# A state scan between two expert mixtures: exponent products over 120 rows, a rebuilt preparation, three state buffers

## The reference

```
xn = rmsnorm(x); delta_lo, Bs, Cs = split(xn @ x_proj_w.T, [8, 8+64])
delta = softplus(delta_lo @ dt_proj_w.T + dt_proj_b);  A = -exp(A_log)       # [128, 64]
# the 2 x 1024 rows are cut into M = 32 chunks of 64 rows, and all chunks step together:
def step(h, (dt, bt, ct, xt)):                         # h: [M, 128 d, 64 n], 64 steps
    h = exp(dt[..., None] * A) * h + dt[..., None] * bt[:, None, :] * xt[..., None]
    return h, einsum('mdn,mn->md', h, ct)
x = x + (y + xn * D) @ out_proj_w.T
```

## Time and profile before

| | us |
|---|---|
| median of 3 runs (1643.73 to 1649.44) | 1645.05 |
| profiled execution | 1653.65 |
| its span | 1651.6 |
| stage d, relu mixture (892.3 to 1022.1) | 129.8 |
| scan, preparation and first steps (1022.1 to 1157.4) | 135.3 |
| scan, the other steps (1157.4 to 1496.9) | 339.5 |
| mixture f (1496.9 to 1651.6) | 154.7 |

### The profile page before, as it was taken

One profiled execution on the slowest core, in us unless ns is written; L12 is line 12 of the kernel. 1 busy time (PEld: TensorE's weight loads), 2 busy tenths in 40 slices (PEclk: granted clock), 3 DMA queues, 4 the chain that ended last, 5 costly groups with the idle time before them and its releaser, 6 DMA issues.

```text
span 1651.6 us, 30294 instructions
## 1 busy us (share of the span) xinstructions
PE 1370.3 (83%) x11160; PEld 917.5 (56%) x11160; DVE 1037.8 (63%) x2050; ACT 958.5 (58%) x1507; POOL 649.1 (39%) x520
## 2 busy tenths in 40 slices
PE   4889996699999987889999996714888888877998
PEld 2667774344444434657666774413666666655676
DVE  5887766877777755786675445513666666665533
ACT  4667773166666676767675442534677677653433
POOL 2756656711222003756553002503566666661000
PEclk9999998699999997999999998755555555557999
DMA  4100000000000000010000000134111101110000
GB/s 139 53 25 1 0 1 1 1 1 2 2 0 1 1 1 26 26 53 1 0 1 1 1 0 0 21 69 73 46 26 25 25 22 25 31 53 1 1 0 25
DMA packets 34316, 32.20 MB, mean 19 GB/s; under 512 B 24200, under 2 KB 27672, under 8 KB 32536
## 3 DMA queue, kind: packets, MB, share of 16 engines
q1 hardware_dynamic: 34200, 30.64, 7.5%
HBM read 24.81 MB, written 5.82 MB: 19 GB/s over the span
## 4 chain that ended last, share of the span: by engine, by line
PE 56%; DVE 14%; ACT 13%; issue 8%; SPq 5%; POOL 2%; DMA 1%; DVEq 0%; POOLq 0%; ACTq 0%
PE ps L595 12%; PE ps L672 7%; PE ps L895 7%; PE ps L682 7%; ACT arena L1149 6%; PE ps L787 4%; PE ps L750 4%; PE ps L868 3%; PE ps L770 3%; DVE maxima L1667 3%; ACT hr L1038 2%; DVE xn L1468 2%; SPq L505 2%; PE ps L881 1%; SPq L499 1%
## 5 line engine op out<-in xcount | busy, mean ns | idle before, releaser
L1149 ACT ACTIVATE arena<-ps 128x512 f32<-128x512 f32 x256 | 244.5, 1080 | 116.4 <-PE ps L868 116.1
L1387 POOL TENSOR_TENSOR arena<-arena 128x512 f32<-128x512 f32 x126 | 223.4, 1793 | 194.9 <-PE ps L895 83.8
L1667 DVE TENSOR_REDUCE maxima<-ps 128x1 f32<-128x512 f32 (+3 forms) x320 | 190.3, 633 | 59.4 <-PE ps L753 39.9
L868 PE MATMUL ps<-arena 12*128 12x64 bf16 x2048 | 136.5, 236 | 101.0 <-DMA arena<-dt_parts 52.8
L595 PE MATMUL ps<-xp,wup 128*128 128x512 f32 (+1 forms) x768 | 207.8, 418 | 13.9 <-ACT hr L1038 10.0
L1411 POOL TENSOR_TENSOR hr<-arena,hr 128x512 fp32r<-128x512 f32 x128 | 173.7, 1363 | 93.8 <-ACT hr L1038 93.6
L595 PE MATMUL ps<-hr,wdn 128*128 128x512 f32 x768 | 201.3, 412 | 8.8 <-DVE hr L1570 7.3
L1104 ACT ACTIVATE arena<-ps 128x1024 f32<-128x1024 f32 (+1 forms) x192 | 150.5, 812 | 73.2 <-PE ps L770 37.0
L1038 ACT ACTIVATE arena<-ps 128x512 f32<-128x512 f32 x256 | 162.5, 635 | 51.0 <-PE ps L595 50.6
L868 PEld LDWEIGHTS ps<-arena 12*128 12x128 bf16 x2048 | 103.7, 121 | 157.1 <-ACT arena L1149 77.1
L595 PEld LDWEIGHTS ps<-xp,wup 128*128 128x128 f32 x768 | 148.3, 200 | 64.3 <-POOL wup L1398 16.4
(11 more groups left out here) (206 smaller groups left out, 2162.6 us busy)
## 6 DMA issues: line engine op xcount, KB each, us to landing
arena<-up_dram SPq DMA_DIRECT2D x16, 256.0 KB, 2.9
arena<-dn_dram SPq DMA_DIRECT2D x16, 256.0 KB, 3.2
arena<-up_dram SPq DMA_DIRECT2D x2, 1024.0 KB, 4.9
arena<-dn_dram SPq DMA_DIRECT2D x2, 1024.0 KB, 7.8
b_parts<-arena SPq DMA_DIRECT2D x16, 96.0 KB
dt_parts<-arena SPq DMA_DIRECT2D x8, 192.0 KB
u_parts<-arena SPq DMA_DIRECT2D x16, 96.0 KB
arena<-dt_parts SPq DMA_DIRECT2D x32, 48.0 KB
```

What stands on the lines that cost most here:

```text
L868: mm = e.matmul(ps[:, 4 + n % 2, j * 64:(j + 1) * 64], aw[32 * r:32 * r + KR, g0 + j, :], dts[k % 2][32 * r:32 * r + KR, g0 + j, :, th * T ...
L1149: e.activation(to.rearrange("p t m d -> p d m t"), ps[:, 4 + n % 2, :].rearrange("p (d m t) -> p d m t", d=DBK, t=TU), ACT.Exp, scale=-1.0 ...
L1387: e.tensor_tensor(hs[:, t % 2, cols], decay[:, u % 2, t4 * W + cols.start:t4 * W + cols.stop], hs[:, 1 - t % 2, cols], ALU.mult).then_inc( ...
L1667: e.tensor_reduce(maxf[:, at_max[0]:at_max[-1] + 1:max(1, at_max[-1] - at_max[0])], ps[:, n % 2, 0:ng * w].rearrange("p (g k) -> p g k", g ...
```

## The change

The diff touches only the scan, what GpSimd does in stage d, and what SP loads.

- The stationary tile of the exponent product has up to 120 rows (10 channels x 12 rows, zero outside the 12 rows of the channel) x 128, for each of the 128 channels; the moving tile holds the 10 channels' dt rows in one block of 120 rows. Products, columns and banks stay in number. `aw` grows from 4096 to 16384 bf16 a partition and is loaded by 60 DMAs in place of 24.
- The decay ACTIVATE reads the bank with a hop of 64 words from element to element and writes runs of 8 adjacent words.
- The input products of banks 2 and 3 are issued together, after the third addition of a step.
- The state has three buffers (t % 3); the multiply waits for the outputs of step t-3.
- POOL's memsets of `aw` and `czf` go to the head of stage d; that of bparts is gone.
- B is computed with padded weights `xpb`, so that its rows come out in the order of time; the splitting is shared out anew (POOL: B only; ACT: casts; DVE: subtractions), the skip product and the transposes of xn come later.
- The stores become few and large: one for b, one for dt, three small ones for the first dt chunk (dt0), two and two for u. The first dt chunk is fetched with two DMAs, further ones with 30 each; u and b are fetched in chunks of 4 steps with 24 DMAs.

The core of it:

```diff
         def spread_bank(e, n):
...
             for j in range(DBK):
-                mm = e.matmul(ps[:, 4 + n % 2, j * 64:(j + 1) * 64], aw[32 * r:32 * r + KR, g0 + j, :],
-                              dts[k % 2][32 * r:32 * r + KR, g0 + j, :, th * TU:(th + 1) * TU], start=True, stop=True)
+                d = q * DBK + j
+                nk = KR * min(DG, D - d // DG * DG)
+                of = dts[k % 2][0:nk, d // DG, :].rearrange("p (m t) -> p m t", t=TC)
+                mm = e.matmul(ps[:, 4 + n % 2, j * 64:(j + 1) * 64], aw[0:nk, d, :],
+                              of[:, :, th * TU:(th + 1) * TU], start=True, stop=True)
...
         def scan_tensor(e):
...
-                if t + 1 < NSTEP:
-                    e.wait_ge(SC["added"], 3 * t + 2)
-                    inputs(e, t + 1, (2,))
                 for n in todo[2:3]:
                     spread_bank(e, n)
                 e.wait_ge(SC["added"], 3 * t + 3)
                 if t + 1 < NSTEP:
-                    inputs(e, t + 1, (3,))
+                    inputs(e, t + 1, (2, 3))
                 state_out(e, t)
...
         def decay_bank(e, n):
...
-            to = decay[:, u % 2, :].rearrange("p (t m d) -> p t m d", t=TU, d=D)[:, :, :, d0:d0 + DBK]
-            e.activation(to.rearrange("p t m d -> p d m t"),
-                         ps[:, 4 + n % 2, :].rearrange("p (d m t) -> p d m t", d=DBK, t=TU), ACT.Exp,
+            to = decayf[u % 2].rearrange("p (t m d) -> p t m d", t=TU, d=D)[:, :, :, d0:d0 + DBK]
+            e.activation(to, ps[:, 4 + n % 2, :].rearrange("p (d m t) -> p t m d", d=DBK, t=TU), ACT.Exp,
                          scale=-1.0).then_inc(SC["decay_ready"], 1)
...
             def decay_state(t):
...
-                if t >= 2:
-                    e.wait_ge(SC["y_done"], t - 1)
+                if t >= 3:
+                    e.wait_ge(SC["y_done"], t - 2)
...
+            def relu_mixture_pool(e, st, nxt):
+                if nxt and nxt["kind"] == "scan":
+                    e.wait_ge(MX["y_read"], len(gelus) * NTB * E)
+                    e.memset(czf, 0.0).then_inc(SC["zeroed"], 1)
+                    e.memset(aw, 0.0).then_inc(SC["zeroed"], 1)
```

And SP's new fetches:

```diff
+                def fetch_dt(k):
+                    for dg in range(DG):
+                        ng = len(range(dg, D, DG))
+                        for c0, na in RUNS:
+                            r0 = KR * dg + 2 * c0
+                            sp.dma_start(dts[k % 2][r0:r0 + 2 * na, 0:ng, :],
+                                         scratch["dt"][dg::DG, k, 0:2 * na, :].rearrange("g r n -> r g n")
+                                         ).then_inc(dt_in[k % 2], 16)
...
+                fetch_inputs(0)
+                for m2 in range(2):
+                    sp.dma_start(scratch["u"][m2, TI:CHUNK].rearrange("t a b h n -> t a (b h n)"),
+                                 uparts[m2 * CHUNK + TI:(m2 + 1) * CHUNK]).then_inc(u_out, 16)
+                sp.wait_ge(u_out, 16 * 2)
+                fetch_inputs(1)
+                sp.wait_ge(dt_out, 16)
+                sp.wait_ge(SC["xn_turned"], NTB)
+                fetch_dt(1)
+                for k in range(2, NI):
+                    sp.wait_ge(SC["in_done"], 3 * TI * (k - 1))
+                    fetch_inputs(k)
+                    if k % 2 == 0 and k // 2 + 1 < NC:
+                        sp.wait_ge(SC["spread_done"], 2 * BKU * (k // 2))
+                        fetch_dt(k // 2 + 1)
```

More of the change, by code:

```diff
@@ new lines, in scan_tensor @@
+            turn_rows(0)
+            turn_rows(1)
+            low_rank(0)
+            turn_rows(2)
+            low_rank(1)
+            steps_of(0)
+            turn_rows(3)
+            low_rank(2)
+            steps_of(1)
+            low_rank(3)
+            steps_of(2)
+            rows_b(0)
+            rows_b(1)
+            steps_of(3)
+            rows_b(2)
+            rows_b(3)
+            for h in range(2):
+                e.wait_ge(SC["bf_ready"], h + 1)
+                for b in range(B):
+                    mm = e.matmul(ps[64 * b:64 * b + 64, 4 + h, :], xpw[:, RANK + STATE:RANK + 2 * STATE],
+                                  ut[:, b * S + h * 512:b * S + (h + 1) * 512], start=True, stop=True)
+                mm.then_inc(SC["bc_done"], 1)
@@ new lines, in scan_tensor @@
+            for g in range(NTB):
+                e.wait_ge(SC["z_added"], g + 1)
+                for j in range(TPB):
+                    mm = e.transpose(ps[:, g, j * P:(j + 1) * P], xn[:, TPB * g + j, :], ident[:])
+                mm.then_inc(SC["xn_turned"], 1)
+            for g in range(NTB):
+                e.wait_ge(SC["u_ready"], g + 1)
+                if g < 2:
+                    e.wait_ge(SC["cT_ready"], g + 1)
+                else:
+                    e.wait_ge(SC["bf_ready"], g + 1)
+                for j in range(TPB):
+                    mm = e.transpose(ps[:, 4 + g, j * P:(j + 1) * P], ut[:, (TPB * g + j) * P:(TPB * g + j + 1) * P], ident[:])
+                mm.then_inc(SC["u_turned"], 1)
@@ new lines, in dt_rest, with u_rest @@
+                def dt_rest(n, g):
+                    e.wait_ge(SC["dt_cast"], n * NTB + g + 1)
+                    for m2 in range(2):
+                        ins = e.tensor_tensor(dt_piece(1, g, m2), dt_piece(n, g, m2), dt_part(n, g, m2), ALU.subtract)
+                    ins.then_inc(SC["dt_rest"], 1)
+                def u_rest(n, g):
+                    e.wait_ge(SC["u_cast"], n * NTB + g + 1)
+                    of = ps[:, 4 + g, :] if n == 0 else urest[:, parts[g]]
+                    e.tensor_tensor(urest[:, parts[g]], of, uparts[:, n, parts[g]], ALU.subtract).then_inc(SC["u_rest"], 1)
@@ new lines, in scan_vector @@
+                z_add(0)
+                for g in range(1, NTB):
+                    z_add(g)
+                    z_size(g - 1)
+                z_size(NTB - 1)
+                for g in range(NTB):
+                    e.wait_ge(SC["ln_ready"], g + 1)
+                    e.scalar_tensor_tensor(out=zt[:, parts[g]], in0=zt[:, parts[g]], scalar=0.0, in1=soft[:, parts[g]],
+                                           op0=ALU.max, op1=ALU.add).then_inc(SC["dt_ready"], 1)
+                e.wait_ge(SC["bc_done"], NTB + 2)
@@ L1781, in scan_vector @@
+                for g in range(NTB):
+                    dt_rest(0, g)
+                    e.wait_ge(SC["dt_ready"], g + 1)
+                    e.tensor_tensor(ut[:, parts[g]], zt[:, parts[g]], ut[:, parts[g]], ALU.mult).then_inc(SC["u_ready"], 1)
+                for g in range(NTB):
+                    dt_rest(1, g)
+                for g in range(NTB):
+                    u_rest(0, g)
+                for g in range(NTB):
+                    u_rest(1, g)
                 e.wait_ge(SC["skip_done"], 1)
```

401 lines of the change are left out of this document (191 added, 210 removed).

## The result

The changed kernel takes 1535.03 us (median of 4 runs, 1533.68 to 1537.93) against 1647.24 of the kernel before on the same chip (4 runs, 1643.73 to 1653.22): ratio 0.9318, 95% interval 0.9285 to 0.9351, so 112 us or 6.8% less. Forecast were 1549 and 96. In the profiled executions the span fell from 1651.6 to 1532.9, by 118.7.

The account below looks back on a forecast made before the run. Scan steps of 5.59 us were taken as bound about equally by TensorE at half clock with its two-buffer wait and by ScalarE's banks. Gains 39 - 12 + 69 = 96 off 1645 gave 1549 us; 8-in-10 range 1520 to 1635.

Parts of the forecast that it names:

- Preparation and first stall: Scan's head until the second dt chunk lands: no memset holding VectorE, earlier casts, fewer SP transfers; gain 39 us.
- Memsets in the mixture: Stage before the scan: GpSimd's moved memsets hold a VectorE instruction and delay TensorE; loss 12 us, between 0 and 14.
- Exponent: Decay ACTIVATE on ScalarE: the new read and write pattern cuts a bank from 1083 ns to 0.64 to 0.70 us.
- slower rival: Decay ACTIVATE: hopping PSUM reads cost about 1.5 us a bank, 6.6 us a step, 1679 us in all; chance 0.07.
- second rival: Scan steps: exponent stays at 1.05 us, clock rises, ScalarE bounds at 4.75 us a step, 1567 us; chance 0.12.
- T: Time of one scan step, counted over 60.7 steps: from 5.59 to 4.45 us, a gain of 69 us.
- Clock: TensorE in the scan: 120-row exponent products lift the granted clock from 0.50 to near 1.00, at least mostly.
- sign in the kernel before: TensorE's clock fell to 0.50 during 8-row products and was back at 0.97 once 128-row products ran.
- first rival: Scan steps: clock stays at 0.50, exponent gets fast, TensorE bounds at 5.25 us a step, 1597 us; chance 0.22.
- Inputs together: Input products of banks 2 and 3 issued in one go on TensorE: zero gain, at worst 0.2 us a step lost.
- Gaps at changes of shape: TensorE switching between 120-row and 12-row products: up to 4 x 0.20 us more a step, less at high clock.
- end of a unit: Scan's multiply waiting for ScalarE's last bank of a unit: adds 0.3 to 0.5 us to a step.

Follow-up runs that it names:

- e5: Kernel before, with the decay ACTIVATE writing runs of 8 words and reading PSUM with a hop of 64 words: 1613.91 us, ratio 0.9798.
- e11: Kernel before, with the input products of banks 2 and 3 issued together after the third addition: 1655.70 us, ratio 1.0057.
- e9: Changed kernel, with the mixture's two memsets started later and the bf16 tile cleared through an fp32 view: 1518.82 us, ratio 0.9237.
- e1: Changed kernel, with the decay ACTIVATE back to reading PSUM in order and writing each word 8 KB apart: 1612.63 us, ratio 0.9778.
- e4: Changed kernel, with exponent products using only the first 12 rows, which computes something else: 1587.29 us, ratio 0.9636.
- e2: Changed kernel, with the input products of banks 2 and 3 issued apart again, as before the change: 1555.04 us, ratio 0.9432.
- e10: Changed kernel, with later memsets through an fp32 view, second dt chunk fetched first, five exponent banks in each of the first six steps: 1493.44 us, ratio 0.9068.
- e8: Changed kernel, with five exponent banks a step instead of four in the first six steps: 1511.18 us, ratio 0.9180.
- e6: Changed kernel, with the two memsets before the scan issued as 24 pieces of 512 fp32 words: 1531.67 us, ratio 0.9271.

## Why the prediction was right

The parts measured, 43.6 - 14.2 + 89.2, add up to 118.6 us between the two profiled executions; the medians differ by 112, and the forecast was 39 - 12 + 69 = 96.

*Preparation and first stall*, forecast 39, measured 43.6. Each link is there: the held tensor_scalar went (8.25 to 0.18 us), the parts of u were ready 10 us earlier from the head (59.5 to 49.6), the landing of u took 7.6 (taken as 8). Mis-sized was the fetch of dt: 30 at 0.34 and not 0.45, 3.3 us less, and its first chunk, 2.9 and not 4; the first 24 fetches of u and b took 9.9 and not 7.4, the last landing 1.6 and not 3. The first exponent product came at 1093.5 and not near 1080, behind the skip product's 32 matrix products (1088.2 to 1093.7); it cost nothing, since the steps wait for the second dt chunk. And the 8.25 us were those of one execution. In e5 and e11, which have the same preparation as the kernel before, the same instruction was let in between the first memset and the second:

```profile
1019.36 4.80 DVE L1759 TENSOR_SCALAR veps<-std 128x16 f32<-128x16 f32 x1
```

So 3.5 of the 43.6 us hang on the profiled execution, which is also one of the longer ones of its kernel (1653.65 us, median 1647.24).

*Memsets in the mixture*, forecast -12, measured -14.2. VectorE was held to the end of the second one; it was the tensor_scalar L1572 (at 894.2) and not the copy three instructions on, so that the loss came out a little over 12. In e9 the scan's head comes at 1019.9 for 1036.2: it was the whole loss.

*Exponent.* 0.64 to 0.70 forecast, 0.597 measured: the hop of 256 B in PSUM costs nothing that shows beside the plain pattern's 635 ns, and going from the old pattern to the new is worth 0.48 us an instruction. The slower rival did not come. But I mis-priced what hangs on it. I had put ScalarE at four times 1083 ns, 4.33 us a step; these instructions overlap at their ends, and 215.5 us for 56 steps are 3.85, so ScalarE's own sum was not what held the old step. And the second rival (long exponent, high clock) stood at T = 4.75 and 1567, where e1, the nearest to that case, is at 5.56 and 1613, at a clock of 0.66 and not a high one. I had taken the longest engine's sum for the step where two engines hand two banks to and fro, and had not seen that the clock would not rise far without the short exponent.

*Clock.* The direction was right, and e4 shows that the clock does not rise without the 120 rows; e1 shows that with them, but with the slow exponent, it gets to 0.66 only. The level (0.84, in alternation) was not near 1.00. The sign in the kernel before was weaker than I had read it: its products of 128 rows begin at 1044.9, and the clock stays at 0.50 until 1055. The first rival stood at T = 5.25 and 1597 (its terms, as written, add up to 5.19); e4, which is that case, has 4.97 and 1587.

*Inputs together*, forecast zero, is the term that failed: it is worth 20 us here (e2). I had judged it by order, not by which products can run side by side, nor by the two changes of kind that it saves.

*Gaps at changes of shape*, up to 4 x 0.20 us feared and less at the high clock: they came. In the starts of single products in the changed kernel's trace it is 0.13 us from the last 120-row product to the first of 12 rows and 0.15 back at the high clock (0.03 and 0.055 between two of a kind), 0.17 and 0.25 at the low one (0.05 and 0.11). That is some 0.1 us for each of the three such changes of a step, 0.3 a step. The timeline hides it, since the ends of products are modelled there: in e10 eight 12-row products start at 1203.96, 0.07 before the shown end of the 120-row ones begun at 1203.63. But sixteen 120-row products put off the next kind by 0.58 us (1205.30 to 1205.88) and eight by 0.33 (1203.63 to 1203.96): eight more cost 0.25, and the rest, 0.08, is the change. In e4, where exponents and inputs both have 12 rows, most changes show no such gap (0.01 to 0.05). The rule of the Trainium skill quoted above (TensorEngine Tiling (Array Packing), Key Properties) is borne out in kind by this; the 0.20 that I had set beside it stands in the trace at the weight load of L895, not at its products.

*T*, forecast 4.45, measured 4.12. The 89 us do not split into independent parts. The exponent's pattern alone gives 34 us (e5). Everything but that pattern gives nothing in the steps (e1, T = 5.56 for 5.59). Everything but the rows gives T = 4.97 (e4), 37 us. All together gives 89. Fast exponent and high clock each need the other: with 12 rows TensorE bounds at its low clock, and with the slow exponent the clock rises to 0.66 only and the hand-over takes the rest. What moved the sum from my 69 to 89 is the 20 of the inputs: without them (e2) T is 4.46, the 4.45 of the forecast. That this fits so well is in part luck. I had 0.3 to 0.5 for the end of a unit and a rest for additions and SP; in e2 the multiply waits 40.8 us for late banks, 0.68 a step, and the first addition 21.4 us for its inputs, 0.36. That SP would hold the steps did not happen: 48 fetches of u and b at 0.30 and 30 of dt at 0.33 make 3.1 us a step.

What would release the multiply was forecast wrongly: not the additions but the unit's last bank (20.5 us, 0.34 a step, which the sum had as the end of a unit). e8 removes it.

Open stays why the clock rises and falls just there in the steady part; the runs show the alternation and its dependence on the rows and on the exponent, no more. Open stays too why the runs of e6 lie so far apart (1517.9 to 1534.1). An execution in which VectorE is let in at an early seam of the memsets would be up to 9 us shorter, but the one of 1517.9 has no profile, so this is not shown.

## What to carry to other kernels

Where two engines pass a few buffers to and fro, price the hand-over and not the longer sum: e1 and the second rival differ by 46 us, for that and for the lower clock. Before products are moved or widened, ask which of them run beside each other in other row groups, and how many changes of kind the order makes; the same order gains in one layout and loses in the other. A long memset on GpSimd cost nothing where VectorE had only scalar_tensor_tensor with an operand in PSUM to do (e9), and nearly all its length where a tensor_scalar within SBUF met it.

## What the runs showed of the hardware that I had not expected

- A memset's time goes by elements, not bytes: 128x16384 bf16 13.75 us, the same bytes as 128x8192 fp32 6.92.
- GpSimd kept VectorE's tensor_scalar out over the seams of memsets in every trace of the changed preparation (14.9 us over one seam; 9.00 over the seams of some twenty pieces, for an instruction of 0.18). But not always: in the kernel before it was let in after the second of three memsets (8.25 us), in e5 and e11, with the same three, after the first (4.80). What decides it, no run shows. tensor_tensor (0.42 us for 256 columns), the reduction (0.42) and scalar_tensor_tensor from PSUM (1.12 for four) ran beside memsets at full speed. The Trainium skill (SBUF — State Buffer, Who interferes with whom) says that copy, cast and tensor_scalar can lock the port pair that both engines share, and that tensor_tensor with two inputs in SBUF is held up only by a GpSimd instruction that reads SBUF. The trace agrees as to the tensor_scalar, and as to tensor_tensor beside a memset; no run here sets apart how it fares beside a GpSimd read.
- A change between products of 120 rows and of 12 costs TensorE some 0.1 us each time (starts 0.13 and 0.15 us apart for 0.03 and 0.055 within a kind, at the high clock), and two products in different row groups start 3 ns apart.
- An ACTIVATE that hops 256 B in PSUM from word to word and writes runs of 8 words takes 597 ns for 512 columns, no more than the plain pattern's 635.
